# A sparse graph network on one core: one variance product per block instead of two, a later wait for the heavy rows, and VectorE taking two of five scaled tiles

## What is computed

```python
# layer 0
adj = adj + eye;  dis = degree ** -0.5
x = layernorm(x + (dis_i * adj * dis_j) @ (x @ W) + bias)          # called h below
# layer 1, for every pair (i, j) with adjacency[i, j] != 0 (about one in 16)
m_j = h @ W1[:D];  m_i = h @ W1[D:]
pre = m_j[:, None] + m_i[:, :, None] + b1
msg = gelu(layernorm(pre, g1, be1))                                 # exact gelu
agg_i = sum_j adjacency[i, j] * msg[i, j]
x = layernorm(h + layernorm(concat(h, agg) @ W2 + b2, g2, be2))
```

## Time and profile before

| | |
|---|---|
| median of 3 runs | 4058.7 us (4058.7, 4040.7, 4058.7) |
| the profiled execution | 4082.1 us, its span 4080.3 us |
| mean granted TensorE clock | 0.974 of full speed |
| steps | 896, about 139.5 us before the first |
| PE / ACT / DVE / POOL busy | 90% / 85% / 78% / 41% |

### The profile page before, as it was taken

One profiled execution on the slowest core, in us unless ns is written; L12 is line 12 of the kernel. 1 busy time (PEld: TensorE's weight loads), 2 busy tenths in 40 slices (PEclk: granted clock), 3 DMA queues, 4 the chain that ended last, 5 costly groups with the idle time before them and its releaser, 6 DMA issues.

```text
span 4080.3 us, 95276 instructions
## 1 busy us (share of the span) xinstructions
PE 3679.1 (90%) x30014; PEld 3304.0 (81%) x30015; DVE 3172.3 (78%) x7110; ACT 3458.4 (85%) x9481; POOL 1665.5 (41%) x1205
## 2 busy tenths in 40 slices
PE   3799999999989989989988999899999989999997
PEld 2688888888868888888887888888888878888887
DVE  2588877788867887778877878778778877878877
ACT  2688888889869888988988888889888989888987
POOL 2344443344433444433444334454334444334431
PEclk8899999999989999999999999999999999999999
DMA  1222221222211222112221122221122221222210
GB/s 34 81 81 84 75 72 43 65 85 84 76 39 57 83 81 78 51 61 67 84 76 63 51 65 84 78 81 55 60 65 85 84 75 51 65 63 84 71 62 16
DMA packets 245631, 276.59 MB, mean 68 GB/s; under 512 B 22320, under 2 KB 204080, under 8 KB 245040
## 3 DMA queue, kind: packets, MB, share of 16 engines
q1 hardware_dynamic: 212272, 168.62, 13.8%
q0 software_dynamic: 32768, 100.70, 6.7%
HBM read 160.17 MB, written 109.05 MB: 66 GB/s over the span
## 4 chain that ended last, share of the span: by engine, by line
PE 57%; ACT 12%; issue 11%; POOL 9%; DVE 7%; DMA 3%; SPq 1%; DVEq 0%; POOLq 0%; ACTq 0%; PEldq 0%
PE z_even_ps L1269 9%; PE agg_even_ps L1232 9%; POOL table L450 8%; PE agg_odd_ps L1232 8%; PE z_odd_ps L1269 8%; ACT tmp L648 3%; PE p_ps L1152 3%; PE p_ps L1153 3%; PE p_ps L1094 3%; PE z_even_ps L1265 2%; PE z_odd_ps L1265 2%; ACT root L579 2%; ACT msg L635 2%; DMA nbr_heavy<-table 1%; DVE pick L1002 1%
## 5 line engine op out<-in xcount | busy, mean ns | idle before, releaser
L648 ACT ACTIVATE tmp<-nbr,r_sb 128x128 f32<-128x128 f32 x4864 | 1519.1, 389 | 29.2
L1002 DVE SCALAR_TENSOR_TENSOR pick<-rank,root_p 128x512 f32<-128x512 bf16 (+3 forms) x1664 | 927.5, 586 | 60.6 <-ACT rank L598 60.6
L1032 DVE SCALAR_TENSOR_TENSOR spread<-rankT,nbr 128x512 f32<-128x512 bf16 (+3 forms) x1664 | 913.1, 577 | 0.0
L450 POOL DMA_INDIRECT table<-stage,row_id x512 | 744.8, 1455 | 337.8 <-issue 301.4
L635 ACT ACTIVATE msg<-msg 128x768 f32<-128x768 f32 (+1 forms) x896 | 726.9, 811 | 35.5 <-issue 32.0
L1232 PE MATMUL agg_odd_ps<-spread,msg 128*128 128x128 f32 x5120 | 656.8, 278 | 35.5 <-issue 18.3
L1269 PEld LDWEIGHTS z_even_ps<-mi_g,pick 128*128 128x128 f32 x5120 | 652.4, 197 | 31.7 <-issue 2.9
L1269 PE MATMUL z_even_ps<-mi_g,pick 128*128 128x129 f32 x5120 | 664.3, 280 | 0.0
L1269 PEld LDWEIGHTS z_odd_ps<-mi_g,pick 128*128 128x128 f32 x5120 | 634.5, 193 | 30.2 <-issue 0.5
L1232 PEld LDWEIGHTS agg_odd_ps<-spread,msg 128*128 128x128 f32 x5120 | 615.5, 194 | 44.2 <-issue 20.1
L1269 PE MATMUL z_odd_ps<-mi_g,pick 128*128 128x129 f32 x5120 | 647.9, 276 | 0.0
(11 more groups left out here) (209 smaller groups left out, 5256.4 us busy)
## 6 DMA issues: line engine op xcount, KB each, us to landing
nbr<-table SPq DMA_DIRECT2D x128, 512.0 KB, 4.0
adj_g<-in_adj SPq DMA_DIRECT2D x32, 1024.0 KB, 5.5
nbr_root<-table SPq DMA_DIRECT2D x128, 256.0 KB, 4.9
nbr_heavy<-table SPq DMA_DIRECT2D x512, 32.0 KB, 3.6
x_g<-in_x SPq DMA_DIRECT2D x32, 256.0 KB, 2.9
table<-stage,row_id POOLq DMA_INDIRECT x512
out<-out_sb SPq DMA_DIRECT2D x32, 256.0 KB, 2.6
w_sb<-in_L_gnn_W SPq DMA_DIRECT2D x2, 128.0 KB, 2.3
```

The source lines that it names most:

```text
L450: pool.indirect_dma_start(table[q], bass.IndirectOffsetOnAxis(ap=row_id[:, jt * TB + it:jt * TB + it + 1], axis=0), stage[:, jt, it, :], N ...
L648: last = act.activation(tmp[:, c % 2, n - FROM[u], :], half_row, ACT.Identity, scale=r_sb[:, c % 2, n - FROM[u]:n - FROM[u] + 1])
L1002: ins = dve.scalar_tensor_tensor(into.rearrange("p k n -> p (k n)"), rank[:, it, span], float(MARK + t), root_p[:, it, span], ALU.is_equal ...
L1032: ins = dve.scalar_tensor_tensor(into, rankT[:, it, jt:jt + count, :], float(MARK + t), nbr[:, it, jt:jt + count, 0:P], ALU.is_equal, ALU. ...
```

## The change

1. **Turned features.** In the setup VectorE turns the centred features (a reflection written as one addition per column) so that the 128th feature of `m_i` and `m_j` is zero. That feature then carries the norm: `mjT`'s row is 1 there (through the activation's bias), and `miT`'s row holds half the sum of `sqi`, since `halves` is now zero but for its last column (0.5) and the product `halves` x `sqi` is made once per graph, at S_MJT, on top of `miT`'s product in the whole bank of `agg_ps[1]`. Each S_V is one fp32 product of 512 columns.
2. **ScalarE's order around it.** `sqi` alone at i = 5 (new semaphore `p_turned` for it, `p_sqi` from it); `miT`, `mjT` and `sqj` at i = 6.
3. **Placement.** The 26 products of 64 columns become 8 of 256, 192, 128, 64 and 256 columns, 1664 columns as before.
4. **Overflow count.** Its four products take bf16 instead of fp32 operands.
5. **Bias of `z`.** The second half of a five-tile unit has 258 instead of 387 columns.
6. **Heavy rows' semaphore.** `nbr_heavy` counts on `t_top[it]`; only VectorE's steps that read heavy rows wait for it, and GpSimd's first scatter waits for it too (four waits more).
7. **Scaled tiles.** In five-tile units ScalarE scales three tiles; VectorE makes the last two messages with one operation each, `half_row * r + z`.

```diff
-                                 table[q][it * N:it * N + HEAVY_W, 0:2 * P]).then_inc(t_read[it], 16)
+                                 table[q][it * N:it * N + HEAVY_W, 0:2 * P]).then_inc(t_top[it], 16)
...
-                                wait_alone(pool, t_read[block_it], (a - 1) * (16 * (1 + HEAVY_T)))
+                                wait_alone(pool, t_read[block_it], (a - 1) * 16)
+                                wait_alone(pool, t_top[block_it], (a - 1) * (16 * HEAVY_T))
...
                 if s == S_MIT:
+                    act.wait_ge(p_turned, a + 1)
+                    act.activation(sqi[:, :], agg_ps[1][:, 0, :], ACT.Square, bias=b1_col[:, :]).then_inc(p_sqi, 1)
+                if s == S_MJT:
                     filled(F_MIT)
-                    act.activation(miT[:, :], p, ACT.Identity, bias=b1_col[:, :])
-                    act.activation(sqi[:, :], p, ACT.Square, bias=b1_col[:, :]).then_inc(p_ev, 1)
-                if s == S_MJT:
+                    act.activation(miT[:, :], agg_ps[1][:, 0, :], ACT.Identity, bias=b1_col[:, :]).then_inc(p_ev, 1)
                     filled(F_MJT)
-                    act.copy(mjT[:, :], p)
+                    act.activation(mjT[:, :], p, ACT.Identity, bias=ident[:, D - 1:D])
                     act.activation(sqj[:, :], p, ACT.Square).then_inc(p_ev, 1)
...
-                    for n in range(FROM[u], FROM[u + 1]):
+                    for n in range(FROM[u], FROM[u] + SCALED[u]):
...
+                    if SCALED[u] < size:
+                        dve.wait_ge(c_r, g + (c + 1))
+                        if SOURCE[FROM[u + 1] - 1] == HEAVY:
+                            dve.wait_ge(t_top[it], (cx.b + (c // GC + 1)) * (16 * HEAVY_T))
+                        for w in range(3, size):
+                            from_j = SOURCE[FROM[u] + w]
+                            half_row = nbr_heavy[:, it, P:2 * P] if from_j == HEAVY else nbr[:, it, from_j, P:2 * P]
+                            dve.scalar_tensor_tensor(msg[:, c % MSGS, w, :], half_row, r_sb[:, c % 2, w:w + 1], z_cols[c % 2][:, 1, w - 3, 0:D],
+                                                     ALU.mult, ALU.add)
+                    dve.wait_ge(c_tmp, g + (c + 1))
+                    if SCALED[u] < size:
+                        last = dve.tensor_tensor(msg[:, c % MSGS, 0:3, :], z_cols[c % 2][:, 0, :, 0:D], tmp[:, c % 2, 0:3, :], ALU.add)
...
+                    for other in range(TB):
+                        mm(into(0), ones_b[:, :], of(above, other, TB), start=(other == 0), stop=False, skip_group_check=True)
+                    for other in range(TB - 1):
+                        mm(into(other + 1), ones_b[:, :], of(alike, other, TB - 1 - other), start=False, stop=False, skip_group_check=True)
+                    mm(p[:, 0:TB * width], before[:, :], alike[:, :, :].rearrange("p k c -> p (k c)"),
+                       start=False, stop=True, skip_group_check=True).then_inc(p_fill, 1)
...
+                    mm(agg_ps[1][:, 0, :], w1_sb[:, 1, :], hT[:, q, :], start=True, stop=False, skip_group_check=True).then_inc(p_turned, 1)
+                if s == S_MJT:
+                    pe.wait_ge(p_sqi, a + 1)
+                    mm(agg_ps[1][:, 0, :], halves[:, :], sqi[:, :], start=False, stop=True, skip_group_check=True).then_inc(p_fill, 1)
+                    mm(p, w1_sb[:, 0, :], hT[:, q, :], start=True, stop=True).then_inc(p_fill, 1)
...
-                        last = mm(p[0:1, it * P:(it + 1) * P], left_p[:, it:it + 1], ident[:, :], start=True, stop=True)
+                        last = mm(p[0:1, it * P:(it + 1) * P], left_p[:, it:it + 1], ident_b[:, :], start=True, stop=True)
...
-                        mm(p, mjT[:, jt * P:(jt + 1) * P], miT[:, :], start=True, stop=False)
-                        mm(p, halves[:, :], sqi[:, :], start=False, stop=True).then_inc(p_fill, 1)
+                        mm(p, mjT[:, jt * P:(jt + 1) * P], miT[:, :], start=True, stop=True).then_inc(p_fill, 1)
...
-                    pe.wait_ge(t_read[at(k)], (n // TB + 1) * (16 * (1 + HEAVY_T)) if isinstance(n, int) else (n - at(k) + TB) * (4 * (1 + HEAVY_T)))
+                    pe.wait_ge(t_read[at(k)], (n // TB + 1) * 16 if isinstance(n, int) else (n - at(k) + TB) * 4)
...
-                        mm(z[:, h, :, :].rearrange("p k w -> p (k w)"), ones_b[:, :], be_split[:, :, :].rearrange("p k w -> p (k w)"),
+                        some = min(3, SIZES[u] - 3 * h)
+                        mm(z[:, h, 0:some, :].rearrange("p k w -> p (k w)"), ones_b[:, :], be_split[:, 0:some, :].rearrange("p k w -> p (k w)"),
```

More of the change, by code:

```diff
@@ L25 @@
 RUNS = 5
+TURN = 1 / (math.sqrt(D) - 1)
 CAPS = (13, 10, 8, 7)
@@ L44 @@
 UNITS = len(SIZES)
+SCALED = tuple(n if n == UNIT else 3 for n in SIZES)
 FROM = tuple(sum(SIZES[:u]) for u in range(UNITS + 1))
@@ L224, in adj_resnorm_kernel @@
         t_root = [sem(f"t_root{k}") for k in range(2)]
+        t_top = [sem(f"t_top{k}") for k in range(TB)]
         t_fill, t_ev, t_edge, t_heavy, t_over = (sem(f"t_{n}") for n in ("fill", "ev", "edge", "heavy", "over"))
```

57 lines of the change are left out of this document (30 added, 27 removed).

## The result

The changed kernel takes 4123.4 us (4121.9 to 4125.3, 4 runs) against 4058.7 before: a ratio of 1.016, 95% interval 1.011 to 1.021. Timed again later, beside other kernels, it was 4130.9 us and 1.018 (1.016 to 1.019). So it is slower by 1.6 to 1.8%, where I had forecast 3940 us and faster. The time and the place are those of the case that I called D and gave 0.05.

A forecast was written before the change was run, and what follows sets the result against it. No engine bounds all of it: PE in variance steps, ACT and DVE in steps 12 to 16, GpSimd's scatters at step 24. From 4058.7 us, 86.5 and the semaphore's 32 came off: 3940 us, 8-in-10 range 3890 to 3995.

The forecast's parts named there:

- D: Rival: step 24 waits over 3 us in every graph, VectorE's added operations holding up GpSimd's scatters; 4132 us; chance 0.05.
- Variance products: Variance steps and step 6: 2.58 us saved a graph, all on the chain; 83 us, bounds 60 and 90.
- rival B: Variance steps: ACT sets the pace instead of PE, costing some 30 us; 3970 us; chance 0.09.
- Bias: Bias of z, eight times a graph: 129 columns less, half of the places on PE's chain; 7 us, bounds 0 and 14.
- placement: The 26 products ahead of T_EDGE: fewer products save 0.12 us a graph; 4 us, bounds 0 and 6.
- overflow count: Step 13: PE's saving is covered by full ACT and DVE; value 0, or 23 us if the cover were gone.
- setup: Ahead of everything: seven dependent VectorE steps cost +2.5 us.
- Scaled tiles: Steps 14 and 15, where DVE is the chain: +0.3 us in half of the graphs; +5 us, bounds +17 and -10.
- Heavy rows' semaphore: Step 24: T_EDGE's 3 us wait becomes 1.1 to 1.5; saves 48 us, 32 in the median run, bounds 0 and 60.

The follow-up runs named there:

- e16: The changed kernel as it is, timed again beside e13 and e14: 4130.9 us, 1.018 of the kernel before.
- e2: The kernel before with the scaled tiles alone (VectorE makes the last two messages of five-tile units): 4248.8 us, 1.049 of before.
- e1: The changed kernel without the scaled tiles (ScalarE scales all five again): 3943.3 us, 0.974 of the kernel before.
- e3: The changed kernel with the heavy rows' reads back on the common semaphore: 4172.9 us, 1.031 of the kernel before.
- e9: The changed kernel with ScalarE scaling all five tiles and the heavy rows' reads back on the common semaphore: 3991.7 us, 0.979 of before.
- e4: The changed kernel; in steps 14 to 22 VectorE waits for its own last pick before building spread: 3909.4 us, 0.966 of before.
- e14: The changed kernel with one added VectorE reduction a step in steps 14 to 22, reading one 128x64 SBUF operand: 4091.6 us, 1.008 of before.
- e13: The changed kernel with one added VectorE addition a step in steps 14 to 22, reading two 128x64 SBUF operands: 4193.2 us, 1.033 of before.
- e12: The kernel before with VectorE's wait for its own last pick in steps 14 to 22, run again: 4010.0 us, 0.983 of before.
- e8: The changed kernel with VectorE's wait for its own last pick in steps 14 to 17 only: 4044.8 us, 0.987 of before.
- e7: The changed kernel with one added VectorE reduction of one column a step in steps 14 to 22, no wait: 4020.8 us, 0.981 of before.
- e5: The changed kernel with VectorE taking the last two tiles only in blocks 0 and 3: 3999.2 us, 0.974 of the kernel before.
- e6: The kernel before with VectorE's wait for its own last pick in steps 14 to 22: 4272.0 us, 1.042 of before.

## Why the prediction was wrong, step by step

**Variance products: right.** Steps 5 to 9 give 2.68 us a graph, 86 us in all, where I had 83 and a small part of z's bias. The window of steps 7 and 8 has PE busy throughout and ACT at 6.37 of 7.13 us, so rival B did not occur. ACT's wait fell to 34.5 us, not quite under the 30 that I had named.

**Bias, placement, overflow count, setup: right within a few us.** Steps 0 to 4 moved by 0.02 us a graph, so nothing of the 4 us for placement shows. For the overflow count PE's 33.2 us fell to 12.5, but steps 10 to 13 did not get shorter, and the wait ahead of it stayed (30.1 to 28.8 us): its cover was what I named. z's first product comes 0.9 us later in the run than before, where I had 2.5 for the setup; but a second trace of the changed kernel (e16) and those of the others, with the same setup, have it anywhere from 138.4 to 144.2 us, so the setup's price is not to be read from this.

**Scaled tiles: this is the step that failed.** I looked for their price where DVE is on the chain, steps 14 and 15, and put +0.3 us a graph there. Those steps cost nothing (+0.02). z's wait for msg rose from 41 us to 53 (32.0 behind L1001 and 20.8 behind L999), near the 50 that I gave. But the price was somewhere else: I took the scatters' length as given and asked only when the first of them starts. It depends on what DVE does beside them: with these two tiles on DVE they take 33 us where they took 26.6 to 29.5, T_EDGE's wait grows from 56 to 164 us, and steps 22 to 24 take 3.89 us a graph more. The term measures +200 us on the kernel before (e2) and about +170 on the rest of the change (e1), not +5.

**Heavy rows' semaphore: the mechanism was right, the setting not.** The wait now names `nbr`, as forecast. (The 57.4 us in 19 waits that I quoted for before are the weight loads' row; PE's own is 56.4 us in 20.) It is worth 1.3 to 1.5% where every graph waits (e3) and about 20 where few do (e9); I had 48 and, for the median run, 32. It could not bring the wait below 1.5 us, because the scatters before it had grown by 3.6 to 6.4 us; in e1, where they had not, all but the first and the last of the twelve waits are 0.4 to 1.7 us.

Without the scaled tiles my sum reads 3935 us. e1's ratio applied to 4058.7 gives 3952 (3940 to 3964). So the rest of the working was good to some 17 us, and one term spoiled it.

**Why rival D had only 0.05.** I had its place and its price: scatters 4 us longer give 4132 us, and it came to 4123 with 33 us for 26.6 to 29.5. That the two times are so near is partly luck: I had steps 22 to 24 cost 5.0 us a graph more, and they cost 3.9. Its mechanism I had only by half. I said that sixteen more operations a graph hold up descriptor writing. There are sixteen new ones, but eight additions go, so eight more; and they do not hold it up themselves, since e4 has them all and its scatters take 22.2 us. What I did with the rival was wrong as well. The Trainium skill (SBUF — State Buffer, Who interferes with whom) says that a VectorE instruction with at most one SBUF input, outside the two-port modes, does not contend with GpSimd. The new operation takes one tile from SBUF and z from PSUM, and I concluded that D could not happen. As to the operation itself the traces agree with the rule: the scatters get in at it (of those over 1.05 us, 28 end 0.87 to 0.96 us after L995's start on `z_even_ps` and another 28 on `z_odd_ps`), and e14 and e13 differ as it says. But I asked of the new operation only whether it blocks. I should have asked what it does to the others: DVE's stretch of two-operand work became gapless (busy 7.34 of 7.34 us in steps 14 and 15, 7.11 of 7.32 before), and DVE no longer waits for ScalarE there, as it did for 0.21 us in step 15 before, since it has become later and ScalarE was relieved by the same edit. That pause was an entrance for GpSimd, and 18 long scatters of before ended at one. The trace of before had the signs: scatters of 0.96 us beside others of 3.03, and a 3.67 us pick, which I read as a rarity.

What is not settled: why, before, 66 long scatters ended at boundaries between two-operand operations that show no pause, and only 5 after. They are the larger part of what the change closed. A pause too short for the records would explain it. It wasn't tested. So the runs show that the two tiles lengthen the scatters (e1, e2), that a wait of 0.2 us a step undoes it (e4), and at which operations GpSimd gets in (e13, e14); that the tiles do their harm by closing pauses is seen in 18 places and argued for the rest.

## A version that beats both

e4's kernel, run twice: 3909.4 us, 0.966 of before (0.963 to 0.969), and 3909.5 us, 0.959 (0.956 to 0.961). It is the changed kernel with one wait a step in steps 14 to 22. The same wait in the kernel before gave 0.983 and 0.987 in two sets and 1.042 in a third, with the unexplained idle times; the changed kernel with the wait has been timed only in two sets (e1 to e4, e9 to e12) in which no kernel had them. With the wait in steps 14 to 17 only it did have them (e8), so the gain is shown where they stay away.

## What to carry to other kernels

Before moving work to an engine, look at which other engine's long operations end when that engine pauses; a wait that "costs nothing" there may be what a neighbour lives on. On this chip GpSimd's scatters beside a busy VectorE should be read as one pair of timelines: if the long ones all end a fixed time after VectorE pauses or reads one operand, put such a point into every step, and measure it, since a wait shortened the 16 scatters by 11 us here and an added operation with one operand only by 1 to 3 (e4, e7, e14). And when a rival has its mechanism, place and price written out, a rule about one instruction is not enough to dismiss it.

## What the runs showed of the hardware

- A wait of 0.19 us on VectorE in each of nine steps shortened 16 scatters from 33.0 to 22.2 us; a scatter that is let in at once takes 0.96 us, and one that waits ends 0.87 to 0.96 us after the start of a VectorE operation that reads PSUM or one operand (203 of 209 in the changed kernel, 102 of 186 in the kernel before).
- An added VectorE operation of 0.2 us made the kernel 1.0% faster than its base with one SBUF operand and 1.5% slower with two (e14, e13, e16).
- After a 6.09 us wait PE's granted clock averaged 0.60 for 6.75 us of unbroken work, then was 1.00; the same products took 6.08 us there and 3.44 us at a clock of 1.00.
- One program took 4272 us in one set of runs and 4010 us in two others, with idle times of 1 to 5 us on PE, ScalarE and VectorE for which the trace names nothing in the program, only in the steps with scatters. They appeared in one set of runs, in kernels whose scatters take 22 to 24.4 us (e5, e6, e8). Their cause is open.
